# Graph network of four layers: one-hot buffers and PSUM banks for the partial sums of the first and last layer

## The reference

```python
x = ln(x + segment_sum(edge_weight[:, None] * x[src], dst))          # layer 0
x = ln(x + gat(x, edge_index, ...))                                  # layer 1: attention, 8 heads
x = ln(x + mlp_messages(x, edge_index, edge_attr_64, ...))           # layer 2: two-layer MLP on each edge
# layer 3: mean of the neighbours, three gated branches
nsum = segment_sum(feat[src], dst)
h_neigh = where(deg > 0, nsum / max(deg, 1), 0)
fs = feat @ w_self + b_self; fn = h_neigh @ w_neigh + b_neigh
low, high, identity = relu(fs + fn), relu(fs - fn), relu(feat @ w_id + b_id)
x = ln(x + 3.0 * (att(low) * low + att(high) * high + att(identity) * identity))
```

## Time and profile before

| | |
|---|---|
| median of 3 runs | 5934.14 us |
| lowest, highest | 5932.01, 5943.96 us |
| profiled execution, span of the core | 6037.9 us |
| its granted TensorE clock | 0.59 of full speed in layer 0, 0.58 in layer 3 |
| PE, DVE, ACT, POOL busy | 53%, 40%, 18%, 56% of the span |

### The profile page before, as it was taken

How to read it: one execution, slowest core, us unless ns; L and a number is a source line. 1 busy time by engine, 2 the same in 40 slices (tenths; PEclk the granted TensorE clock), 3 DMA queues, 4 the chain that set the end, 5 groups by cost and what they waited for, 6 DMA issues and landing times.

```text
span 6037.9 us, 78867 instructions
## 1 busy us (share of the span) xinstructions
PE 3212.4 (53%) x18493; PEld 2857.5 (47%) x18493; DVE 2438.4 (40%) x9382; ACT 1105.3 (18%) x3073; POOL 3386.5 (56%) x3514
## 2 busy tenths in 40 slices
PE   3433334434677777777436776676773334333344
PEld 2322233323666666667326666666662323323333
DVE  5444444453455555555433333333335212222227
ACT  1111111111222222222111111111113111111114
POOL 6666666555555555555465555555544666666662
PEclk6556665566776767677558988888885555665556
DMA  5363333313555455555135555555541333333331
GB/s 120 99 173 87 88 87 89 86 45 95 130 136 132 131 132 133 136 136 131 50 87 152 152 148 150 149 149 147 152 122 47 83 86 89 87 87 91 90 78 37
DMA packets 899758, 664.43 MB, mean 110 GB/s; under 512 B 109871, under 2 KB 829405, under 8 KB 899566
## 3 DMA queue, kind: packets, MB, share of 16 engines
q10 hardware_dynamic: 495632, 295.95, 17.6%
q0 software_dynamic: 113792, 229.18, 15.7%
q1 hardware_dynamic: 290142, 137.51, 8.2%
HBM read 414.27 MB, written 247.94 MB: 110 GB/s over the span
## 4 chain that ended last, share of the span: by engine, by line
another core or an unknown queue 30%; issue 19%; PE 19%; DVE 15%; ACTq 5%; ACT 5%; DVEq 3%; POOL 2%; DMA 1%; SPq 0%; POOLq 0%
PE bank L511 17%; DVE onehot L1081 3%; DVE lo L1095 3%; PE bank L516 2%; DVE hi L1094 2%; ACTq L767 2%; ACT part_s L763 2%; DVEq L1077 1%; ACTq L787 1%; DVE onehot L1084 1%; ACT part_s L760 1%; POOL agg L473 1%; ACT hid L877 1%; ACTq L793 1%
## 5 line engine op out<-in xcount | busy, mean ns | idle before, releaser
L511 PE MATMUL bank<-g,onehot 128*128 128x128 f32 x3136 | 700.7, 399 | 1222.8 <-DVE onehot L1081 399.7
L511 PEld LDWEIGHTS bank<-g,onehot 128*128 128x128 f32 x3136 | 619.1, 296 | 1301.6 <-issue 589.1
L431 POOL DMA_INDIRECT g<-xl,srcq x784 | 756.4, 965 | 693.3 <-ACT srcq L776 477.3
L431 POOL DMA_INDIRECT g<-a_src,srcq x784 | 764.0, 974 | 604.4 <-ACT srcq L776 348.6
L431 POOL DMA_INDIRECT g<-x,srcq x784 | 746.7, 952 | 449.3 <-issue 231.7
L431 POOL DMA_INDIRECT g<-in_x,srcq x784 | 747.1, 953 | 433.9 <-issue 226.4
L1084 DVE TENSOR_SCALAR onehot<-iota_row,crec 128x128 f32<-128x128 f32 x2352 | 526.7, 298 | 936.7 <-remote 733.9
L511 PE MATMUL bank<-onehot_t,work 128*128 128x128 f32 x3136 | 732.5, 327 | 0.0
L516 PE MATMUL bank<-ident,g 128*128 128x128 f32 x1568 | 521.2, 332 | 352.5 <-DVE onehot_t L1104 178.3
L511 PE MATMUL bank<-msg,onehot 128*128 128x144 f32 (+1 forms) x3136 | 559.7, 331 | 190.5 <-issue 186.9
L511 PEld LDWEIGHTS bank<-onehot_t,work 128*128 128x128 f32 x3136 | 620.9, 245 | 0.0
(11 more groups left out here) (299 smaller groups left out, 4591.9 us busy)
## 6 DMA issues: line engine op xcount, KB each, us to landing
partial<-part_s ACTq DMA_DIRECT2D x588, 256.0 KB
partial<-part_s ACTq DMA_DIRECT2D x196, 288.0 KB
work<-local_rank ACTq DMA_DIRECT2D x392, 128.0 KB
work<-xr_by_rank SPq DMA_DIRECT2D x784, 64.0 KB
work<-b_by_rank SPq DMA_DIRECT2D x784, 64.0 KB
work<-in_rel_t ACTq DMA_DIRECT2D x196, 128.0 KB
g<-in_x,srcq POOLq DMA_INDIRECT x784
g<-xl,srcq POOLq DMA_INDIRECT x784
```

What stands on the lines that cost most here:

```text
L431: pool.indirect_dma_start(g[:, s * TQ + t, :], None, table, bass.IndirectOffsetOnAxis(srcq[:, s * TQ + t:s * TQ + t + 1].bitcast(U32), 0), ...
L511: return nc.tensor.matmul(to, lhsT, rhs, start=start, stop=stop, skip_group_check=True)
```

## The change

Layers 0 and 3 get rings in place of pairs. One-hots: 7 buffers in both (layers 1 and 2 keep 2). PSUM banks for the sums: seven in layer 0 (4, 5, 6, 7, 0, 1, 2), four in layer 3 (4, 6, 5, 7). The histogram's one-hots get 7 buffers too. DVE waits for the sum of the quad seven before, PE for the copy of the quad seven or four before. Memory for it comes from sharing: the 7 one-hots lie over `onehot_t`, `slope` and `hid`, which only layers 1 and 2 use; the histogram's lie in the memory of `chain_m`, so DVE waits for all counts before it builds `chain_m`, no longer after `penc`. Layer 3's own projections lose banks 5 and 7: they are done in two halves (4 and 3 blocks) on banks 2 and 3, with a step of PE and one of ACT more, a new semaphore from ACT to PE (`half_split`), and steps up to 27. The semaphore `partial_done` starts at 7 instead of 2, and its other waiters' offsets follow.

```diff
+FILLS = RING
+ONEHOT_RING = {0: 7, 1: 2, 2: 2, 3: 7}
+PARTIAL_BANKS = {0: (4, 5, 6, 7, 0, 1, 2), 2: (4, 6), 3: (4, 6, 5, 7)}
...
-        chain_m = sb("chain_m", [TP, CH * (CH + 1) // 2, TP])
+        chain_buf = sb("chain_buf", [P, CH * (CH + 1) // 2, TP])
+        chain_m = chain_buf[0:TP]
...
-        onehot = sb("onehot", [P, 2, TQ, P])
-        onehot_t = sb("onehot_t", [P, 2, QE])
-        hi1 = sb("hi1", [P, 2, TQ, NB], BF16)
-        lo1 = sb("lo1", [P, 2, TQ, P], BF16)
-        slope = sb("slope", [P, 2, QE])
-        hid = sb("hid", [P, 2, QE])
+        quads = sb("quads", [P, 8, QE])
+        onehot = quads[:].rearrange("p r (t e) -> p r t e", e=P)
+        onehot_t, slope, hid = quads[:, 2:4, :], quads[:, 4:6, :], quads[:, 6:8, :]
+        hist_b = chain_buf[:].rearrange("p c e -> p (c e)").bitcast(BF16)
+        hi1 = hist_b[:, 0:RING * TQ * NB].rearrange("p (r t e) -> p r t e", t=TQ, e=NB)
+        lo1 = hist_b[:, RING * TQ * NB:RING * TQ * (NB + P)].rearrange("p (r t e) -> p r t e", t=TQ, e=P)
...
-        def part_ps(l, r, t):
+        def partial_bank(l, q):
+            return bank[PARTIAL_BANKS[l][q % len(PARTIAL_BANKS[l])]]
+
+        def part_ps(l, q, t):
 
             if l == 1:
                 return bank[4 + t // 2][:, (t % 2) * ROWW:(t % 2 + 1) * ROWW]
-            return bank[4 + 2 * r][:, t * D:(t + 1) * D]
+            return partial_bank(l, q)[:, t * D:(t + 1) * D]
...
-        (STEP_STATES, STEP_FLIP, STEP_COLUMNS, STEP_PROJECT, STEP_SPLIT, STEP_DOTS, STEP_ROOT, STEP_SCORE,
-         STEP_EXP, STEP_ELU, STEP_EXP2, STEP_MIX) = range(1, 25, 2)
+        (STEP_STATES, STEP_FLIP, STEP_COLUMNS, STEP_PROJECT, STEP_SPLIT, STEP_PROJECT2, STEP_SPLIT2, STEP_DOTS,
+         STEP_ROOT, STEP_SCORE, STEP_EXP, STEP_ELU, STEP_EXP2, STEP_MIX) = range(1, 29, 2)
...
-        OWN_BANKS = (2, 3, 5, 7)
+        OWN_BANKS = (2, 3)
+        OWN_ROWS = (range(0, 4), range(4, BT))
...
-            pe.sem_inc(partial_done, 2)
+            pe.sem_inc(partial_done, FILLS)
+            pe.sem_inc(hist_done, RING)
...
-                    i, r = n * QB + q, q % 2
+                    i, r = n * QB + q, q % ONEHOT_RING[l]
...
-                    pe.wait_ge(partial_copied, at + (2 if l == 1 else 1))
+                    pe.wait_ge(partial_copied, FILLS + at + 1 - (1 if l == 1 else len(PARTIAL_BANKS[l])))
                     for t in range(TQ):
-                        last = mm(part_ps(l, r, t), onehot[:, r, t, :], rhs_of(q, t))
+                        last = mm(part_ps(l, q, t), onehot[:, r, t, :], rhs_of(q, t))
...
             sweep(pe, [(sum_partials(0, gathered_rhs, None), 0), (count, 0)])
 
+            pe.wait_ge(partial_copied, FILLS + NQ)
...
-                if q == STEP_PROJECT:
-                    pe.wait_ge(xt_copied, 3 * NBAT + b + 2)
-                    for r in range(BT):
-                        to = bank[OWN_BANKS[r // 2]][:, (r % 2) * 2 * D:(r % 2 + 1) * 2 * D]
-                        mm(to, ht7[:, r, :], w_x[:], stop=False)
-                        last = mm(to, ones[0:1, :], b_x[:], start=False)
-                    last.then_inc(z_done, 1)
+                for half, at in enumerate((STEP_PROJECT, STEP_PROJECT2)):
+                    if q == at:
+                        if half == 0:
+                            pe.wait_ge(xt_copied, 3 * NBAT + b + 2)
+                        else:
+                            pe.wait_ge(half_split, b + 1)
+                        for r in OWN_ROWS[half]:
+                            to = bank[OWN_BANKS[r % 4 // 2]][:, (r % 2) * 2 * D:(r % 2 + 1) * 2 * D]
+                            mm(to, ht7[:, r, :], w_x[:], stop=False)
+                            last = mm(to, ones[0:1, :], b_x[:], start=False)
+                        last.then_inc((half_done, z_done)[half], 1)
...
+            def split(b, k, c):
+                z = bank[OWN_BANKS[k % 2]][:, 0:c * 2 * D].rearrange("p (r f) -> p r f", f=2 * D)
+                nc.scalar.copy(own[:, bass.ds(b * BT + 2 * k, c), :], z[:, :, 0:D])
+                return nc.scalar.activation(y7[:, 2 * k:2 * k + c, :], z[:, :, D:], ACT.Relu)
...
                 if q == STEP_SPLIT:
+                    act.wait_ge(half_done, b + 1)
+                    act.wait_ge(mix_read, b + 1)
+                    for k in range(2):
+                        last = split(b, k, 2)
+                    last.then_inc(half_split, 1)
+                if q == STEP_SPLIT2:
                     act.wait_ge(z_done, 3 * NBAT + b + 2)
-                    act.wait_ge(mix_read, b + 1)
-                    for k in range(4):
...
+                    for k in range(2, 4):
+                        split(b, k, 2 if k < 3 else 1)
...
-                    dve.wait_ge(partial_done, NQ * l + i + 1)
+                    dve.wait_ge(partial_done, FILLS + NQ * l + i + 1 - ONEHOT_RING[l])
...
-                i, r = n * QB + q, q % 2
+                i, r, to = n * QB + q, q % 2, q % RING
...
             v.tensor_copy(lnb3[:], lnb[:, 0:1].broadcast_to([P, 3])).then_inc(prep_dve, 1)
+            dve.wait_ge(hist_done, RING + NQ)
...
-            dve.wait_ge(hist_done, NQ + 2)
```

More of the change, by code:

```diff
@@ L241, in gnn_program @@
             sem(n) for n in ("norm_ready", "xt_done", "xt_copied", "z_done", "node_out"))
+        half_done, half_split = sem("half_done"), sem("half_split")
         update_read, rel_cleared = sem("update_read"), sem("rel_cleared")
@@ L517, in flip @@
                                         skip_group_check=True)
-            pe.sem_inc(partial_done, 2)
+            pe.sem_inc(partial_done, FILLS)
+            pe.sem_inc(hist_done, RING)
             for l in (1, 2):
                 pe.sem_inc(expanded[l], RING)
-            for s in (alpha_done, max_t_done, hidden_used, hist_done):
+            for s in (alpha_done, max_t_done, hidden_used):
                 pe.sem_inc(s, 2)
@@ L738, in _ @@
         def _(act):
-            act.sem_inc(partial_copied, 2)
+            act.sem_inc(partial_copied, FILLS)
             act.sem_inc(alpha_copied, 2)
@@ L837, in project_out @@
                 rows_out(layer, NBAT - 1)
-            sweep(act, [(refill(partial_done, 2), 0), (put_partials(0), 0)])
+            sweep(act, [(refill(partial_done, FILLS), 0), (put_partials(0), 0)])
             act.wait_ge(hist_dve, 3)
@@ L944, in own_columns @@
                         gate(z_id, k, 3 * b + k)
-            sweep(act, [(refill(partial_done, 3 * NQ + 2), 0), (put_partials(3), 0)], 2, own_columns)
+            sweep(act, [(refill(partial_done, 3 * NQ + FILLS), 0), (put_partials(3), 0)], 2, own_columns)
             def mix_rows(b):
```

28 lines of the change are left out of this document (12 added, 16 removed).

## The result

| | before | after |
|---|---|---|
| median of 7 runs | 5938.04 us | 5911.07 us |
| lowest, highest | 5929.49, 5961.08 us | 5894.69, 5930.55 us |
| ratio after / before | | 0.995, 95% interval 0.9931 to 0.9968 |
| profiled execution, span | 6037.9 us | 5909.3 us |

The account below looks back on a forecast made before the run. It took layers 0 and 3 as bound by POOL's gathers at 1.25 us plus stalls from held completions. From 5934 us, -94 - 82 - 0 - 5 = -181 us gave 5753 us; overall range 5580 to 5946.

Parts of the forecast that it names:

- Term (1): Layer 0: seven one-hot and histogram buffers and seven banks give 8 quads per stall, 25 stalls fewer, -94 us.
- wrong altogether: Sign against the forecast: POOL waiting over 6 us several times per layer 3 batch, or late completions holding ACT's or DVE's semaphores.
- Term (2): Layer 3: seven one-hots and four banks give 8 quads per stall, 24.5 stalls for 50, -82 us.
- Term (3): Layer 3's own projections in two halves on banks 2 and 3: cost 0, covered by POOL's lead of 7 quads.
- Rival D: Slower: a hold of 22.4 us falls on PE's second-half wait in each layer 3 batch, 5992 us; chance 0.08.
- Term (4): Layer 0's end, where chain_m waits for the last count: net 0, between -5 and +5 us.
- Term (5): Layer 3's end: one hold of 7.7 us among the last sums would fall, -5 us, between 0 and -8.
- Term (6): Layers 1 and 2 keep two buffers and two banks: 0.
- its own range: The forecast case's range for the whole kernel: 5680 to 5825 us, stalls cut to a third or by a third.
- B: Layers 0 and 3: holds last until POOL is quiet, or hardly exist without the profiler; no change, 5929 us; chance 0.12.
- C: Layers 0 and 3: only five to six quads per stall, 33 to 39 stalls for 50, -69 us, 5865 us; chance 0.15.
- A: Layers 0 and 3: holds have a length of their own, stalls all but vanish, -353 us, 5581 us; chance 0.20.

Follow-up runs that it names:

- f1: The changed kernel, unedited, on a chip without holds: 4798.36 us against 4788.52 for the kernel before, ratio 1.0023.
- e1: The kernel before, unchanged, profiled once more as a base for comparing stages: 5943.66 us.
- g3: The changed kernel with short fills on POOL, without a drain, after each quad in layer 0 and each gather in layer 3, holding chip: 5903.51 us.
- g2: The changed kernel with a lead of 14 quads instead of 7 in layer 0, on a holding chip: 5939.51 us.
- e4: The changed kernel with layer 3's rows read by SyncE with plain DMAs of consecutive rows instead of POOL's indirect ones: 5293.58 us.
- g1: The kernel before, unchanged, profiled on another chip, which holds completions: 5943.50 us.
- k1: The changed kernel with two one-hot buffers and banks 4 and 6 everywhere, so without its rings: 5941.45 us, ratio 0.9994 to before.
- e3: The changed kernel with every sum's four matmuls done twice in layers 0 and 3: 5970.83 us.
- g4: The changed kernel without layer 0's histogram but for one quad, and four one-hots per DVE instruction in layer 3, holding chip: 5931.85 us.
- h1: The changed kernel with partial sums stored in another row order, in runs of 2048 bytes: 5904.15 us, ratio 0.9937 to before.
- e2: The changed kernel with a fill and drain on POOL after each quad in layer 0, a drain after every gather in layer 3: 7773.77 us.
- e7: The changed kernel with the edits of g4, on a chip without holds: 4867.72 us.

## Why the prediction was wrong

**What bounds the kernel** was read rightly as far as the rows went: POOL at 1.25 us a gather plus stalls, which end when ACT sees a sum complete. On two of the other chips the stalls are absent (f1).

**Term (1), layer 0, -94 us: -9 to -13 measured. This is the step that failed**, in two places. First, "PE may now issue every sum whose gather has landed ... the release completes up to 6": 3 in fact. The prediction took the hold for one of PE's completions only, and let DVE and PE run ahead at full speed ("their one-hots are made and their sums mostly issued"). After shows both crawling, a sum per 13.3 us, and only three quads of one-hots made in 39 of 46 stalls. It had named late signals of DVE as what would make it wrong altogether, but looked for none. Before hardly shows them: with two buffers DVE itself waits for a held sum during most of a hold. Of the 1372 steps from one small instruction of DVE to the next within a quad, one is over 0.6 us in e1, and 116 are in after.

Second, and worse, the sum was stalls times a fixed price. Stalls have no fixed price: g3 cut them to 30 waits of 2.8 us and g2 left 38 of 4.2 us, at nearly the same length. What stays nearly the same on a holding chip, as long as the other engines' work does, is the time that POOL is away from its gathers. Not counting the 0.30 us between two gathers, it is 163.7 us in layer 0 of after, 162.7 in g2, 163.2 in g3 with its fills and 156.2 in e4; with pairs it is 177.6 (e1), 174.8 (g1) and 170.1 (k1). With twice the matmuls (e3) it is 188.6 us, with the histogram left out (g4) 139.4. That they pay for the other engines' instructions, at 7 to 11 ns each, fits these runs but isn't shown; at 8 ns it would be 7601 x 0.008 = 61 us, and the other 100 us (an estimate: 1147.8 - 980 - 61 = 107) would have a cause that no run varied. More buffers took away only what POOL stood still beyond that. That was 9 to 13 us.

**Term (2), layer 3, -82 us: -6 to -13 measured.** The same step. "A quad is 8 matmuls, 10 us when held" was read from one interval, and the next one there, 5313.45 to 5326.78, is 13.3 us; with twice the matmuls (e3) it should have been 20, and the sweep grew by 0.14 us a quad.

**Term (3), the halves: 0 forecast, none seen** (k1, 0.9979 to 1.0008). Rival D, a hold on `half_split`, didn't come.

**Term (4), layer 0's end: 0 within 5 forecast**, 226.8 us after against 226.1 and 230.1.

**Term (5), layer 3's end: -5 forecast, -8 measured** (208.0 against 216.0 and 216.7), but e3 and h1, with the same rings, have 214.9 and 214.0, and the first profile of before has 210.9. It can't be told from scatter, so the agreement is no more than luck.

**Term (6), layers 1 and 2: 0**, and they lie within or beside the two profiles of before.

**The sum.** The base was a further fault: 202.0 us of waits in layer 0 came from an execution that was 104 us slow throughout; in e1's and g1's kind it is 174. The text saw the 104 us and didn't scale. By the same sum, with g1's 48 waits of 3.6 us and 45 of 3.5 us, it would still have been some -150 us. The edges of its own range are rough too: with the two prices, stalls cut by a third are 5813 us and cut to a third 5697, not 5825 and 5680.

**The rivals.** B had the right kind of reason, "the holds last until POOL is quiet and the engines catch up no further than now", at 5929 us, 18 above the result; its other reason, that the holds hardly exist without the profiler, was tested by no run (f1's chip has none with it). C had the right count, five quads per stall, at 5865 us, 46 below it: with five quads 50 stalls become 39, and 40 were found, but each was 0.4 us longer. Its sum has a slip besides: 33 to 39 stalls for 50 in both layers, at 3.74 and 3.22 us, are -77 to -118 us, and -69 is ten stalls fewer. A's condition, a hold of limited length, was refuted by g2. The measured time lies in the range of 5580 to 5946, but that range takes in no change at all.

## What to carry to other kernels

When engines wait for each other's signals while nobody is busy, find out what total has to be paid before counting stalls: insert pauses of known size, and if the length doesn't change (g3), removing stalls one by one is worth little, and more buffers return at most what is left above the total. Before costing a buffer ring, look for every engine that shows the same symptom: a ring that isn't filled gains little (after), and where DVE did fill it, PE was the slow one (g3). Run before on a second chip: a fifth of this kernel's time went with the chip.

## What the runs showed of the hardware

The same program takes 5934 to 5946 us on some chips and 4789 us on others (in these groups three holding chips and two without holds). All but one of the chips were met in one group only, so whether a chip keeps to its kind isn't known. Where completions are held, records are missing as well: the trace of after has 2,799 records of signals by DMAs in layer 0's sweep, that of f1 16,421, with the same DMAs. The Trainium skill ("NOTIFIC — the notification-queue block", Overflow: three behaviours, one of which stalls the engine) says that the block which writes such records passes its own back-pressure on to the engines rather than lose a record inside. Engines that slow down by a few ns per recorded instruction would fit that; that records are missing doesn't. No run here was made without recording, so whether the holds exist without it stays open, and so does why a chip has them.

POOL's stream of indirect DMAs, one per 1.25 us, goes with holds of some 20 us on such a chip (ACT's refill waits 19.72 us at 1048.97 in after); with a pause of 2.6 us behind each quad (e2), or with plain DMAs by SyncE in its place (e4), they are gone.

With a drain on POOL between indirect DMAs the idle time between two of them grows from 0.30 to 2.3 to 2.6 us (e2, layer 3).

One DVE instruction with a broadcast over 512 elements in place of four saved 43 us of DVE's time in layer 3 (g4, 213.10 for 255.82 us) and lengthened POOL's gathers by 18.6 us; on a chip without holds the gathers took 777.13 us for 753.15, and the sweep went from 991.8 to 1015.8 us (e7, f1). The Trainium skill ("SBUF — State Buffer", Who interferes with whom) says that a DVE instruction with two SBUF inputs contends with a GpSimd instruction that reads SBUF; the two runs agree in direction, though they don't separate the second input from the greater length of the instruction.
